# Product-key memory attention on one Trainium2 core: ten of 32 heads by dense lookup instead of eight, and a new order of the quads

## The reference

```
def _pk(x, Wq_pk, pk_keys):                       # 8 heads, 64 keys on each of 2 sides
    q = (x @ Wq_pk).reshape(b, n, 2, HEADS, 32).transpose(2, 0, 1, 3, 4)
    sim = einsum('pbnhd,pkhd->pbnhk', q, pk_keys)
    scores, idx = top_k(sim, 16)                  # per side
    score = scores[0][..., :, None] + scores[1][..., None, :]     # 16 x 16 pairs
    final_scores, pk_idx = top_k(score, 16)
    final_scores = softmax(final_scores)
    ...
q = (x @ Wq).reshape(b, n, HEADS, 64) * 64 ** -0.5
kv_scores, indices = _pk(x, Wq_pk, pk_keys)
k = einsum('bnhk,bnhkd->bnhd', kv_scores, keys_table[ind])        # 4096 rows per head
v = einsum('bnhk,bnhkd->bnhd', kv_scores, values_table[ind])
attn = softmax(causal(einsum('bihd,bjhd->bhij', q, k)))
out = einsum('bhij,bjhd->bhid', attn, v) -> ... @ Wo
```

## Time and profile before

| what | us |
|---|---|
| median of 3 runs | 14013.33 (14011.51 to 14019.07) |
| the profiled execution | 14017.65 |
| its span, first to last instruction | 14015.6 |
| first gather of l3m starts | 5841.52 |
| last gather of l3m ends | 13774.35 |
| busy over the span: PE / DVE / ACT / POOL | 9358.8 / 9539.3 / 6297.5 / 7987.4 |

### The profile page before, as it was taken

One profiled execution on the slowest core, in us unless ns is written; L12 is line 12 of the kernel. 1 busy time (PEld: TensorE's weight loads), 2 busy tenths in 40 slices (PEclk: granted clock), 3 DMA queues, 4 the chain that ended last, 5 costly groups with the idle time before them and its releaser, 6 DMA issues.

```text
span 14015.6 us, 129357 instructions
## 1 busy us (share of the span) xinstructions
PE 9358.8 (67%) x34236; PEld 4949.2 (35%) x34236; DVE 9539.3 (68%) x21923; ACT 6297.5 (45%) x13845; POOL 7987.4 (57%) x6892
## 2 busy tenths in 40 slices
PE   1556455455545655277887877877877877877777
PEld 0343122122213122134444434444444444444444
DVE  3332988888883874777777676677777677776751
ACT  0111333334321012156666666666666666666653
POOL 3000566666650000277777777777777777777772
PEclk9655777777775776578887888878888888888886
DMA  1000222222220000111222212212222112112220
GB/s 25 1 14 3 92 102 97 97 98 97 103 90 10 12 8 6 29 51 52 58 52 53 56 51 55 55 51 56 53 52 57 52 52 57 52 51 58 52 52 23
DMA packets 305053, 730.88 MB, mean 52 GB/s; under 512 B 130242, under 2 KB 170737, under 8 KB 269914
## 3 DMA queue, kind: packets, MB, share of 16 engines
q0 software_dynamic: 201216, 405.72, 11.1%
q1 hardware_dynamic: 103178, 317.81, 6.7%
HBM read 706.25 MB, written 8.42 MB: 51 GB/s over the span
## 4 chain that ended last, share of the span: by engine, by line
POOL 38%; issue 12%; PE 5%; DVE 2%; ACT 1%; DVEq 0%; DMA 0%; POOLq 0%; ACTq 0%
POOL l3m_got L2239 38%; PE l3m_O L2308 1%; PE l3m_S L2291 1%; PE l3m_T L2298 1%; PE l3m_acc L2334 1%; PE l3m_DX L2324 0%; ACT l3m_spread L2430 0%; ACT l3m_probT L2465 0%; ACT l3m_prob L2456 0%; PE l3m_T L2278 0%; DVE l3m_hot L2596 0%; DVEq L2592 0%; PE l3m_T L2265 0%; DVE l3m_hot L2593 0%; DVE l3m_hot L2589 0%
## 5 line engine op out<-in xcount | busy, mean ns | idle before, releaser
L2239 POOL DMA_INDIRECT l3m_got<-in_l_table,l3m_row x6144 | 6036.4, 982 | 1938.9 <-issue 1868.7
L2430 ACT ACTIVATE l3m_spread<-l3m_got,l3m_weight 128x128 f32<-128x128 f32 x6136 | 2109.6, 490 | 437.8 <-DMA l3m_got<-in_l_table,l3m_row 432.5
L2334 PE MATMUL l3m_acc<-l3m_W,l3m_values 128*128 128x512 f32 x2048 | 1343.8, 744 | 142.8 <-ACT l3m_W L2473 138.4
L1262 POOL TENSOR_TENSOR m_mul<-m_st,m_wide_c 128x2048 f32<-128x2048 f32 x256 | 1157.4, 4521 | 150.0 <-DVE m_st L1415 143.8
L2308 PE MATMUL l3m_O<-l3m_vo_g,l3m_probT 128*128 128x64 f32 x6528 | 1003.9, 299 | 317.7 <-ACT l3m_probT L2465 306.3
L2308 PEld LDWEIGHTS l3m_O<-l3m_vo_g,l3m_probT 128*128 128x128 f32 x6528 | 950.8, 215 | 723.7 <-ACT l3m_probT L2465 643.0
L2465 ACT ACTIVATE l3m_probT<-l3m_T 128x512 f32<-128x512 f32 (+3 forms) x1280 | 692.9, 541 | 1005.9 <-PE l3m_T L2298 1003.9
L2291 PE MATMUL l3m_S<-l3m_kvT_g,l3m_qT 64*128 64x512 f32 (+3 forms) x1920 | 751.2, 755 | 575.0 <-ACT l3m_prob L2456 561.4
L1295 PE MATMUL m_W<-m_mul,tower_ident 128*128 128x512 f32 (+1 forms) x1536 | 836.9, 667 | 206.9 <-POOL m_mul L1262 205.9
L2677 DVE SCALAR_TENSOR_TENSOR tower_h<-l3m_O,l3m_pinv,tower_h 128x64 f32<-128x64 f32 x512 | 145.4, 284 | 1195.1 <-PE l3m_O L2308 1173.6
L2469 ACT ACTIVATE l3m_V<-l3m_DX,l3k_least 128x512 bf16<-128x512 f32 x1024 | 699.5, 683 | 429.7 <-PE l3m_DX L2318 421.5
(11 more groups left out here) (677 smaller groups left out, 18538.4 us busy)
## 6 DMA issues: line engine op xcount, KB each, us to landing
m_wide_c<-l1a_c SPq DMA_DIRECT2D x256, 1024.0 KB, 4.7
l3m_got<-in_l_table,l3m_row POOLq DMA_INDIRECT x6144
l3m_values<-in_l_table SPq DMA_DIRECT2D x32, 512.0 KB, 3.9
l0i_img<-in_l_x SPq DMA_DIRECT2D x4, 1024.0 KB, 8.0
l2r_x<-l2a_hT SPq DMA_DIRECT2D x8, 512.0 KB, 5.5
qp_inw<-in_q_inw SPq DMA_DIRECT2D x1, 2336.0 KB, 7.8
l_kept<-l0t_xt,l0t_row POOLq DMA_INDIRECT x128, 2.2
l1a_c<-m_mul SPq DMA_DIRECT2D x16, 128.0 KB, 2.6
```

Source lines behind the costliest of these rows:

```text
L1262: pool.tensor_tensor(mul[:, k % 2], st[:, k % 2], wide_c[:, k % CRING], ALU.mult).then_inc(multiplied, 1)
L2239: pool.indirect_dma_start(got[:, unit % GOT, j, :], None, table, bass.IndirectOffsetOnAxis(ap=row[:, unit // QUAD % RING, unit % QUAD, j:j ...
L2334: pe.matmul(acc[:], values[:, tile, :], W[:], start=(tile == 0), stop=(tile == TILES - 1)).then_inc(blended, 1)
L2430: last = act.activation(spread[:, unit % 2, :, j], got[:, unit % GOT, j, :], ACT.Copy, scale=weight[:, g % RING, t, j:j + 1])
```

## The change

Heads 5 to 7 of sequences 0 and 2 and heads 6 and 7 of sequences 1 and 3 are dense: 10 heads (40 quads), and 22 (88 quads) are gathered. The rows of 16 steps are gone; there are 537 steps numbered by `s`, and three lists say what stands where: `pick_order` (quads sorted by a due step), `attend_order` (PERIOD, BEFORE: ahead of which gathered quads a dense one stands), and even rates. In every step 11 copies are done (5632 / 512) and two pieces or three in turn (1280 / 512). `held`, by which every fourth gathered quad was made one step later, is gone. The loops over slots on PE and ACT are written anew; on DVE `share` and the two subtractions stand behind `top_pairs`, and `store` at the slot in which the last piece is blended.

```
-DENSE = 2
-GATHER = HEADS - DENSE
+GATHERED = (5, 6, 5, 6)
+PERIOD, BEFORE = 44, (0, 4, 6, 8, 10, 12, 14, 16, 18, 20, 24, 26, 28, 30, 32, 34, 36, 38, 40, 42)
+LAG, UNITS_FROM, PIECES_FROM = 6, 12, 8
...
+COPIES = TOPK * GQ // QUADS
...
+def first_piece(s):
+    return TILES * DQ * (s - PIECES_FROM) // (QUAD * QUADS)
+
+def pick_order():
+    def due(kind, i):
+        if kind == "g":
+            return UNITS_FROM + QUAD * TOPK * i / COPIES - 6
+        return PIECES_FROM + QUAD * QUADS * i / DQ - 9
+    return sorted([("g", i) for i in range(GQ)] + [("d", i) for i in range(DQ)], key=lambda x: (due(*x), x[0]))
...
+    def copies(s):
+        j = COPIES * (s - UNITS_FROM - 1)
+        return range(max(j, 0), max(min(j + COPIES, QUAD * TOPK * GQ), 0))
...  (PE)
-                    for c in range(max(3, depth[n] // 4 + 1)):
-                        if c <= depth[n] // 4:
-                            flip(n, c)
-                        if todo and c == 0:
-                            cross(todo[0])
-                        if todo and c == 1:
-                            onward(todo[1])
-                        if todo and c == 2:
-                            cross(todo[1])
-                        if c <= depth[n] // 4:
-                            mixing(n, c)
+                for c in range(max(chunks, len(todo))):
+                    if c < chunks:
+                        flip(n, c)
+                    if c < len(todo):
+                        cross(todo[c])
+                    if c < chunks:
+                        mixing(n, c)
+                    if c + 1 < len(todo):
+                        onward(todo[c + 1])
...  (ACT)
+                part_up(mine[0:share])
+                for c in range(max(chunks, len(todo))):
+                    if c < chunks:
+                        take_flip(n, c)
+                    if c < len(todo):
+                        grow(todo[c])
+                    part_up(mine[(c + 1) * share:(c + 2) * share])
+                    if c + 1 < len(todo):
+                        lift(todo[c + 1])
...  (DVE)
                     top_pairs(kind, t, p % 2)
+                d = dense_picked(s, 6)
+                if d is not None:
+                    dve.wait_ge(highd, d + 1)
+                    dve.tensor_tensor(shown[:], shown[:], high[:, d % 2, :], ALU.subtract).then_inc(leftd, 1)
+                d = dense_picked(s, 7)
+                if d is not None:
+                    dve.wait_ge(midd, d + 1)
+                    dve.tensor_tensor(tail[:, d % 2, :], shown[:], mid[:, d % 2, :], ALU.subtract).then_inc(taild, 1)
+                past, end = pick_at(s - 2)
+                if end == QUAD - 1:
+                    share(past)
```

More of the change, by code:

```diff
@@ new lines, in copies, with unit_summed, dense_picked, made_at @@
+    def copies(s):
+        j = COPIES * (s - UNITS_FROM - 1)
+        return range(max(j, 0), max(min(j + COPIES, QUAD * TOPK * GQ), 0))
+    def unit_summed(s):
+        ends = [j // TOPK for j in copies(s - 1) if j % TOPK == TOPK - 1]
+        return ends[0] if ends else None
+    def dense_picked(s, by):
+        p, t = pick_at(s - by)
+        return picks[p][1] if t == 0 and picks[p][0] == "d" else None
+    def made_at(s):
+        n = tile_at(s + 2)
+        return kinds[n] if n is not None and n % QUAD == 0 else None
@@ L2363, in _ @@
                 if todo:
                     onward(todo[0])
-                elif r == ROWS and q == 0:
-                    blend(TILES * ROWS - 1)
-                made = made_at(r, q)
-                held = made is not None and made == nxt
-                if nxt is not None and not held:
+                elif pieces(s - 1):
+                    blend(TILES * DQ - 1)
+                if nxt is not None:
                     scores(nxt)
+                chunks = depth[n] // 4 + 1 if n is not None else 0
@@ L2684, in store @@
                     dve.wait_ge(placed, g)
-                dve.wait_ge(t_taken, T_at["inverse", g - 1] + 1)
+                dve.wait_ge(t_taken, T_at["inverse", g] + 1)
                 dve.tensor_tensor(stage[:], acc[:], invT[:, g % 2, :], ALU.mult).then_inc(staged, 1)
-            for r, q in steps:
-                n = number.get((r, q))
+            for s in range(STEPS):
+                n = tile_at(s)
+                todo = pieces(s)
+                done = [(i, k // TILES - 1) for i, k in enumerate(todo) if k and k % TILES == 0]
+                if not todo and pieces(s - 1):
+                    done = [(0, DQ - 1)]
+                when, held = done[0] if done else (None, None)
```

373 lines of the change are left out of this document (164 added, 209 removed).

## The result

The changed kernel takes 14305.86 us (median of 4 runs, 14261.99 to 14314.34), the kernel before 14012.42 in the same series: a ratio of 1.0202 [1.0189, 1.0215], slower. Two further series gave 1.0192 [1.0175, 1.0209] and 1.0209 [1.0195, 1.0223]. The prediction was 13900, so the time is 406 us above it, and 56 us above the range.

A forecast was written before the change was run, and what follows sets the result against it. POOL's gathers were taken to bound the kernel before, and the chain of steps through PE, ACT and DVE the changed one. Terms of -432.5 -175 +813 +102 -165 +34 -290 summed to -114, giving 13900 us, range 13370 to 14250.

The forecast's parts named there:

- waits ahead of the copies: ScalarE's waits for gathers, 432.5 us in 98 places, go if the PE, ACT and DVE chain is the bound: -432.5.
- copies: On ACT, 32 units less are 512 copies fewer, 0.343 us each: -175.
- 256 pieces: Added pieces on PE and ACT, 128 at 2.5 us and 128 alone at 3.85: +813.
- new slots: Only a flip now stands between a piece's level and its cross: 0.4 us in 256 deep steps, +102.
- picks, clock and all else of the layout: Dense picks -165, ACT's work for them +34, PE's clock -290, and DVE's moved small steps 0.
- the clock: PE's loss of 1064 us at 1.2 GHz shrinks by 27% as waits for gathers go: -290, ends 0 and -1064.
- the picks: ACT's wait for DVE's maximum in dense picks falls from 8.5 to 2.7 us each, for 40 picks: -165.
- their work: ACT's own work for a dense pick, 4.3 us, eight times more: +34.
- POOL stays the bound: Rival: POOL's gathers still set the layer's time, 13373 us; chance 0.13.
- The slower rival: Shallow steps, depth 0 to 7, fall to 1.2 GHz on PE: 14170 to 14446, time 14200; chance 0.32.
- VectorE's picks: Rival: DVE's dense picks set the pace, 8.5 us of wait staying in each of 40: 14130; chance 0.05.

The follow-up runs named there:

- eight heads in the same slots: Changed kernel's layout with eight dense heads instead of ten, blend and level before the mixing and cross behind it from the second slot: 14041.32 us, 1.0006 of the kernel before.
- the last pair: Changed kernel beside itself with blend and level before the mixing, cross behind it, from the second slot, on one chip: 14311.79 and 14069.65 us.
- ten heads with the lift under the mixing: Changed kernel with blend and level ahead of the mixing and cross behind it from the second slot on: 14069.65 us, 1.0037 of the kernel before.

## Why the prediction was wrong

**What held.** POOL's first gather starts at 5884.1 (predicted 5885.0). POOL waits hundreds of us. The gathers' waits of ScalarE go. The subtractions' fall from 269.3 us to 109.7 (66.1 for `shown`, 43.6 for `tail`), which is not the "near zero" that was foretold. The wait for the maximum is 67.2 (predicted 108, before 272.7). A lone piece at full clock was priced at 3.85 us, and the trace of after has 3.84 from cross to cross, 8090.30 to 8094.14, with only a mixing beside it while ScalarE grows. Rows of PE from its timeline:

```profile
8090.30 0.39 PE L2332 MATMUL l3m_DX<-l3m_high,l3k_sel 128*128 128x512 bf16 x1 [0.56 <-ACT l3m_V L2466]
...
8092.02 1.12 PE L2342 MATMUL l3m_acc<-l3m_W,l3m_values 128*128 128x512 f32 x2 [0.30 <-ACT l3m_W L2470]
...
8094.14 0.39 PE L2332 MATMUL l3m_DX<-l3m_high,l3k_sel 128*128 128x512 bf16 x1 [0.78 <-ACT l3m_V L2466]
```

The steps that got a third piece, against eight heads in the same slots, grew by 2.42 and 2.68 us with one copy less (0.34), so 2.8 and 3.0 a piece where the sum had 3.2. What the higher clock gave back in these steps is in that price.

**What failed, term by term** (us; the measured column is an estimate from the table of steps, with the changed kernel of the last pair; the slots are measured against those of ten heads with the lift under the mixing, not against those of the kernel before; the last term is what is left over):

| term | predicted | measured |
|---|---|---|
| waits ahead of the copies | -432.5 | -365 |
| copies | -175 | -175, not told apart |
| 256 pieces | +813 | +742 (2.9 each) |
| new slots | +102 | +313 |
| picks, clock and all else of the layout | -421 | -204 |
| sum | -114 | +311 (profiled: +315, and +285 for the first run) |

*The new slots* are the step that the pair of runs shows to have failed: 211 us more than the term (+313 for +102). The sentence that failed is "I count 0.4 us in the 256 deep steps; in the shallow ones nothing stood there before either". For deep steps it was near (0.53 measured). In the shallow ones something did stand there: ScalarE's share of copies, between `lift` and `grow` of the second piece. The change puts it behind that `grow`. I followed only what TensorE has beside the lift, and not what ScalarE has beside the cross. The rows for it were at hand, since the earlier trace rows give `grow` 409.4 us of waits for 1024 pieces, 0.40 each; it became 0.75.

*Clock and picks*, the other 217. I had the clock at -290, the picks at -165 and their work at +34. The first two came about in the rows of single engines. By the prediction's own way of estimating, TensorE lost 1064 us to the lower clock at 0.82, and at 0.87 it loses 26% of 6054 us at twice its length, 787, so 277 are won back; and the wait for the maximum fell by 205. But with eight heads in the new layout it had fallen too (150.2), and the steps were no shorter. Of 482 us won in two engines' rows only 204 + 34, about half, are left over for the steps. My reading, not shown: TensorE and ScalarE wait for each other in turn, so that a matmul that ends earlier often only lengthens another wait, and I took two such gains whole. By how much each of them fell short isn't settled, since no run changes one alone. Nearly all of the 204 lies in steps without a third piece: from eight to ten heads with the same slots the first step of a quad fell by 0.49 us and the third, that of the `make`, by 1.69, where the missing copy gives 0.34, and 128 x (0.15 + 1.35) is 192. Why the third step fell so far was not followed.

By the rule of the Trainium skill's page "TensorE: Matmul & The Clock Gate" (Why this matters for your kernels), idle gaps between bursts of matmuls are to be avoided, or the throughput drops to that of half the clock. The traces agree: the clock from 6000 to 13500 is 0.82 in the kernel before and in eight heads with the lift under the mixing, which both wait over 430 us for gathers, and 0.87 in the changed kernel and in ten heads with the lift under the mixing, which hardly do. What the higher clock gives in time no run here isolates.

*The waits ahead of the copies* stay at 70.9 us in the first run, 49.7 of them for VectorE's sum (`kv`), a wait that was 0.8.

**The rivals.** That POOL stays the bound is refuted by its waits; the mean of one gather went from 982 to 987 ns, so its price hardly grew either. The slower rival named the right sign with the wrong cause: it needed the clock under 0.80, and steps at depth 0 to 3 over 15 us; the clock is 0.87 and these steps are 13.88 us long with all waits. VectorE's picks don't set the pace (67.2 us). The 211 us that the slots cost over their term are more than the 113 us over the sum at which, by the prediction, the change is no gain.

## What to carry to other kernels

Where two engines pass a tile to and fro, write the orders of both side by side and ask of each handover what the waiting engine has to do in it. Here a block of free work (three copies, 1.08 us) was worth more between two dependent instructions of ScalarE than behind them: the two placements of the pieces differ by 242 us in 14070. Count that for every step, the shallow ones too. And don't take a gain that is read from the rows of one engine in such a chain as a gain of the chain: here about half was left of it, by a remainder that no run isolates.

## What the runs showed of the hardware that was not expected

The same kernel before took 14029.9 us in one series and 18342.85 in another on the same chip. In the second sort ScalarE's instructions are as long as in the first, TensorE's are somewhat longer at a lower granted clock, and a part of the difference is idle time that no engine's record explains. An example is the kernel before with the slots of the change (the profiled execution took 18529.46 us; groups of instructions):

```profile
L2467 ACT ACTIVATE l3m_V<-l3m_DX,l3k_least 128x512 bf16<-128x512 f32 x1024 | 700.7, 684 | 1806.1 <-remote 1081.4 <-PE l3m_DX L2318 451.7 <-issue 271.0
L2463 ACT ACTIVATE l3m_probT<-l3m_T 128x512 f32<-128x512 f32 (+3 forms) x1280 | 683.8, 534 | 2761.3 <-remote 1534.3 <-PE l3m_T L2298 904.3 <-issue 320.0
```

Lift and flip copy take 684 and 534 ns, as in the first sort (683 in the earlier trace rows, and 541 for the flip copy), but stand idle for 1806 and 2761 us. The first matmul of a cross takes 496 ns where it took 449, with a clock of 0.67 for 0.82 from 6000 to 13500. In that trace TensorE, ScalarE and VectorE are idle together for over 1.5 us in 521 places after 6000, 1906 us in all and up to 13.9 at once, while POOL in most of this time goes on starting a gather every 1.25 us; in the trace of the kernel before there are 17 such places, 58 us. One kernel has a trace of each sort, ten heads with the lift under the mixing: 378 places and 1386 us in one of the second, none in that of the first. The spans of the first two differ by over 4500 us, so this is less than half of it. What holds the engines is open. It matters for reading ratios: ten heads with the other slots are 1.3 to 2.0% faster than the kernel before there, and 0.4% slower in a series of the first sort, since POOL, the bound of the kernel before on the first sort, waits thousands of us on the second (4618.7 in this trace).
